# GpSimd takes the C products of steps 14 and 15 in place of step 8, y in four terms, and the first stage's softmax two row steps earlier

## The reference, cut to what matters

```python
xn = layernorm(x)
# branch 1, a selective scan (N = 16 states)
deltaBC = xn @ W_deltaBC.T                       # 64 + 16 + 16 columns
delta, B, C = split(deltaBC, [64, 80])
delta = softplus(delta @ W_dt.T + b_dt)          # [b, l, 256]
deltaA = exp(delta[..., None] * A)               # [b, l, 256, 16]
BX = delta[..., None] * B[:, :, None, :] * xn[..., None]
hs = scan over l of  h = deltaA * h + BX
y = einsum('blds,bls->bld', hs, C) + D * xn
# branch 2, 8 experts of which each picks its 128 best tokens of every batch
S = softmax(xn @ Wg.T);  G, I = top_k(S^T, 128)
out = G * (gelu(xn[I] @ W1 + b1) @ W2 + b2), added to the rows I
result = x + y + out
```

## Time and profile before

| | |
|---|---|
| median of three runs | 2423.44 us (2422.18 to 2428.61) |
| the profiled execution, device time | 2422.32 us |
| its span in the trace | 2420.4 us |
| granted TensorE clock, mean | 0.987 |
| DVE busy | 2349.7 us (97%) |
| PE busy | 2286.8 us (94%) |
| POOL busy | 2146.5 us (89%) |
| ACT busy | 2074.3 us (86%) |
| DMA, mean | 167 GB/s; near 100% of the engines in the first 120 us, 50 to 65% after |

### The profile page before, as it was taken

The page is one execution under the profiler, slowest core; times in us unless marked ns, Lnnn a source line. Parts: engine busy times, 40 slices in busy tenths (PEclk is TensorE's granted clock), DMA queues, the critical chain, the costliest instruction groups (busy, mean ns, idle before and its releaser), DMA issues. The chain is left out here.

```text
span 2420.4 us, 33772 instructions
## 1 busy us (share of the span) xinstructions
PE 2286.8 (94%) x10756; PEld 1816.4 (75%) x10756; DVE 2349.7 (97%) x1975; ACT 2074.3 (86%) x3629; POOL 2146.5 (89%) x1235
## 2 busy tenths in 40 slices
PE   7749999999999999999999999999999999999996
PEld 4437777777777777777777777777778777777775
DVE  5799999999999999999999999999999999999997
ACT  7748889898888888988888889888898989888884
POOL 5527999999999899999999999999999999999997
PEclk9969999999999999999999999999999999999998
DMA  9967575645656565555656555565646456565444
GB/s 344 338 209 266 158 221 157 177 136 148 168 147 173 145 161 141 165 154 134 184 137 173 136 166 145 141 176 143 177 127 180 127 151 163 149 173 139 128 127 79
DMA packets 151649, 403.04 MB, mean 167 GB/s; under 512 B 19536, under 2 KB 88240, under 8 KB 134832
## 3 DMA queue, kind: packets, MB, share of 16 engines
q1 hardware_dynamic: 84208, 316.72, 38.2%
q0 software_dynamic: 66048, 83.92, 20.6%
q10 hardware_dynamic: 1216, 0.23, 0.0%
HBM read 323.72 MB, written 91.75 MB: 172 GB/s over the span
## 5 line engine op out<-in xcount | busy, mean ns | idle before, releaser
L585 POOL TENSOR_TENSOR ysum<-ysum,prod 128x1024 f32<-128x1024 f32 x415 | 1121.4, 2702 | 20.3 <-DVE prod L1008 12.1
L997 DVE TENSOR_TENSOR_SCAN bank_x<-decay,bank_x 128x1024 f32<-128x1024 f32 x448 | 1024.7, 2287 | 8.9 <-DVE bank_x L936 0.5
L1163 PE MATMUL bank_l<-ext,w_sb 128*128 128x256 f32 x4096 | 968.9, 384 | 28.2 <-ACT og L757 22.6
L1229 PE MATMUL bank_l<-w_sb,hid 128*128 128x256 f32 x4096 | 939.0, 382 | 0.0
L1163 PEld LDWEIGHTS bank_l<-ext,w_sb 128*128 128x128 f32 x4096 | 760.3, 191 | 166.5 <-ACT og L757 31.0
L1229 PEld LDWEIGHTS bank_l<-w_sb,hid 128*128 128x128 f32 x4096 | 767.5, 190 | 130.0 <-issue 29.0
L717 ACT ACTIVATE decay<-delta,a_sb 128x511 f32<-128x511 f32 x1024 | 641.9, 707 | 15.8 <-POOL delta L517 14.6
L936 DVE TENSOR_TENSOR bank_x<-du,bank_b 128x1024 f32<-128x1024 f32 x512 | 617.6, 1206 | 4.7 <-ACT bank_b L748 3.2
L726 ACT ACTIVATE hid<-bank_l,b_all 128x256 f32<-128x256 f32 x1024 | 431.5, 475 | 203.8 <-PE bank_l L1163 200.7
L1008 DVE TENSOR_TENSOR prod<-bank_x,c_all 128x1024 f32<-128x1024 f32 x448 | 544.9, 1216 | 0.1
L540 POOL DMA_INDIRECT out<-og,idx_all x256 | 410.0, 1601 | 43.8 <-POOL ysum L585 42.5
(11 more groups left out here) (117 smaller groups left out, 1958.9 us busy)
## 6 DMA issues: line engine op xcount, KB each, us to landing
c_all<-bc_rows SPq DMA_DIRECT2D x128, 1024.0 KB, 5.1
b_wide<-bc_rows SPq DMA_DIRECT2D x128, 512.0 KB, 4.5
w_sb<-in_w SPq DMA_DIRECT2D x32, 1024.0 KB, 9.3
decay<-in_x SPq DMA_DIRECT2D x32, 512.0 KB, 6.8
xn_rows<-c_all SPq DMA_DIRECT2D x32, 512.0 KB, 6.5
out<-yrow POOLq DMA_DIRECT2D x32, 512.0 KB, 8.5
xr<-xn_rows SPq DMA_DIRECT2D x30, 512.0 KB, 6.0
bc_rows<-prod SPq DMA_DIRECT2D x32, 192.0 KB, 5.1
```

Of the source, the lines that this page charges most:

```text
L585: nc.gpsimd.tensor_tensor(ysum[:, m % 2], first, prod[:, i], ALU.add).then_inc(sum_done, 1)
L997: nc.vector.tensor_tensor_scan(into, decay[:, k % 2, i].rearrange("p c t -> p (c t)"), bank_x[:, s % 2], 0.0, ALU.mult, ALU.add).then_inc( ...
L1163: i = nc.tensor.matmul(bank_l[(q + v) % 2][:, (f % 2) * UT:(f % 2 + 1) * UT], w1_sb[:, e2, hc, f * P:(f + 1) * P], ext[:, v % 2, hc], star ...
L1229: i = nc.tensor.matmul(o, hid[:, w % 2, f, c * K:(c + 1) * K], w2_sb[:, w_par, f], start=False, stop=(f == FC - 1 and c == UB - 1))
```

## The change

Three things are changed.
- `GP_STEPS` is (4, 14, 15) and `KEPT` is (14, 15): POOL makes the products with C of steps 4, 14 and 15, DVE those of the 13 others (before: 14 others). Step 8 becomes an ordinary step: DVE's product, POOL's add. Steps 14 and 15 are scanned into `kept[:, 0]` and `kept[:, 1]`, multiplied there by POOL and not added by it. `kept` no longer alternates from batch to batch, so DVE waits before both scans until PE has turned all of the batch before (`y_tr`, b * 2). POOL has 13 adds and 3 products in a batch, before 14 and 2.
- y is turned in four terms instead of three: ysum, kept 0, kept 1, skip; 16 matmuls per half instead of 12. For the last batch the terms are added one at a time, each as soon as it is there, with one accumulation per half that starts with skip and ends with kept 1; the second half goes to `bank_l[0]`. Two scatters of the last unit move by a step.
- In the first stage `first` stands in the row steps 4g + 3 and takes the group that PE turned in row step 4g + 1 (before: in row step 4g + 5). `second` and the exponential come two row steps earlier too, so do `TURN0` and the start of the top-k rounds: row steps 23 to 31 hold one round each, 32 to 34 two, 35 the last.

```diff
 BODY = 4
-GP_STEPS = (4, 8)
-KEPT = 8
+GP_STEPS = (4, 14, 15)
+KEPT = (14, 15)
 BU = BODY * SLOTS
...
 WIDE = (1, 2)
-TURN0 = HALF + ROWS - 2
-EARLY = {NB - 7: (0,), NB - 6: (1,), NB - 5: (2,), NB - 4: (3,), NB - 3: (4,), NB - 2: (5,), NB - 1: (6,), NB: (7, 8),
-         NB + 1: (9, 10), NB + 2: (11, 12), NB + 3: (13, 14), NB + 4: (15,)}
+TURN0 = HALF + ROWS - 4
+EARLY = {NB - 9: (0,), NB - 8: (1,), NB - 7: (2,), NB - 6: (3,), NB - 5: (4,), NB - 4: (5,), NB - 3: (6,), NB - 2: (7,), NB - 1: (8,),
+         NB: (9, 10), NB + 1: (11, 12), NB + 2: (13, 14), NB + 3: (15,)}
 LEAD = 16
...
         def sums(s):
-            return s - (s + N - 1) // N - (s + N - 1 - KEPT) // N
+            return s - (s + N - 1) // N - sum((s + N - 1 - n) // N for n in KEPT)
         def gp_prods(s):
...
                                 pool.wait_ge(c_in[u % 2], (u // 2 + 1) * 16)
-                                from_, to = (kept[:, m % 2], kept[:, m % 2]) if n == KEPT else (state[:], prod[:, i])
+                                from_, to = (kept[:, n % 2], kept[:, n % 2]) if n in KEPT else (state[:], prod[:, i])
                                 wait(pool, sum_done, sums(s - 2))
...
                                 pool.wait_ge(gp_prod_done, gp_prods(s + 1))
-                            elif s < NB * N - 1:
+                            else:
                                 pool.wait_ge(prod_done, dve_prods(s + 1))
...
                                 first = ysum[:, m % 2]
-                            if n > 0 and n != KEPT and s < NB * N - 1:
+                            if n > 0 and n not in KEPT:
                                 nc.gpsimd.tensor_tensor(ysum[:, m % 2], first, prod[:, i], ALU.add).then_inc(sum_done, 1)
...
                             scatter(u - 1, 1)
-                        if i == 2 and u == NU - 1:
-                            scatter(u, 1)
-                            scatter(u, 0)
+                        if i in (1, 2) and u == NU - 1:
+                            scatter(u, 2 - i)
                         if i == 3 and sl == 0 and there(b - 2, NB) and u < NU:
...
                     b = q * ROWS + r
-                    g, gq = q * 2 + r // GATE, r // GATE % 2
+                    g, gp = q * 2 + r // GATE, (r // GATE + 1) % 2
                     if b == 5:
...
                         nc.scalar.copy(proj[:, (r - 3) % 4], lg_banks[(r - 3) % 2][0:PJ, :]).then_inc(proj_done, 1)
-                    if r % GATE == 1 and there(g - 2, NB // GATE):
-                        act.wait_ge(lsh_done, g - 1)
-                        nc.scalar.activation(lexp[:, gq], lsh[:, gq], ACT.Exp).then_inc(lexp_done, 1)
+                    if r % GATE == 3 and there(g - 1, NB // GATE):
+                        act.wait_ge(lsh_done, g)
+                        nc.scalar.activation(lexp[:, gp], lsh[:, gp], ACT.Exp).then_inc(lexp_done, 1)
             through(rows, NB // ROWS)
...
                 wait(act, delta_done, nb - 1)
-                wait(act, gp_prod_done, gp_prods((nb - 2) * N + KEPT) if nb > 1 else 0)
+                wait(act, gp_prod_done, gp_prods((nb - 2) * N + KEPT[0]) if nb > 1 else 0)
                 wait(act, du_done, nb - 2)
...
                     gq = 1 - gp
-                    first = r % GATE == 1 and there(g - 2, NB // GATE)
-                    second = r % GATE == 3 and there(g - 2, NB // GATE)
+                    first = r % GATE == 3 and there(g - 1, NB // GATE)
+                    second = r % GATE == 1 and there(g - 2, NB // GATE)
                     lg = bank_t[:, 0:TC * GATE * E].rearrange("p (a e) -> p a e", e=E)
                     if first:
-                        dve.wait_ge(lg_tr, g - 1)
-                        nc.vector.reduce_max(lmax[:, gq], lg, axis=AX.X).then_inc(lmax_done, 1)
+                        dve.wait_ge(lg_tr, g)
+                        nc.vector.reduce_max(lmax[:, gp], lg, axis=AX.X).then_inc(lmax_done, 1)
                     if second:
...
                     if first:
-                        dve.wait_ge(lmax_done, g - 1)
-                        nc.vector.tensor_tensor(lsh[:, gq], lg, lmax[:, gq].unsqueeze(2).broadcast_to([P, TC * GATE, E]),
+                        dve.wait_ge(lmax_done, g)
+                        nc.vector.tensor_tensor(lsh[:, gp], lg, lmax[:, gp].unsqueeze(2).broadcast_to([P, TC * GATE, E]),
                                                 ALU.subtract).then_inc(lsh_done, 1)
...
                         dve.wait_ge(bx_done, s + 1)
-                        if n == KEPT:
-                            wait(dve, y_tr, b * 2 - 2)
-                            into = kept[:, par].rearrange("p c t -> p (c t)")
+                        if n in KEPT:
+                            wait(dve, y_tr, b * 2)
+                            into = kept[:, n % 2].rearrange("p c t -> p (c t)")
                         elif n in GP_STEPS:
...
             dve.wait_ge(y_added, (NB - 2) * 16)
-            nc.vector.tensor_copy(yrow[:, (NB - 1) % 2, 2:4], bank_x[:, 0, 0:T].rearrange("p (c d) -> p c d", c=2)).then_inc(yrow_done, 1)
+            nc.vector.tensor_copy(yrow[:, (NB - 1) % 2, 2:4], bank_l[0].rearrange("p (c d) -> p c d", c=2)).then_inc(yrow_done, 1)
         @block.tensor
...
                 pe.wait_ge(skip_done, y + 1)
-            def y_rows(par, half, last=False):
-
-                into = bank_x[:, 0, 0:T] if last and half else bank_t[:]
+            def y_rows(par, half):
+
                 for c in (2 * half, 2 * half + 1):
                     for dt in range(HC):
-                        part = into[:, (c % 2) * D + dt * P:(c % 2) * D + (dt + 1) * P]
+                        part = bank_t[:, (c % 2) * D + dt * P:(c % 2) * D + (dt + 1) * P]
                         rows = slice(c * P, (c + 1) * P)
-                        terms = [ysum[:, par, dt, rows], kept[:, par, dt, rows], skip[:, par, dt, rows]]
-                        if last:
-                            terms.append(prod[:, STEPS - 1, dt, rows])
+                        terms = (ysum[:, par], kept[:, 0], kept[:, 1], skip[:, par])
                         for t, term in enumerate(terms):
-                            o = nc.tensor.matmul(part, term, ident[:], start=(t == 0), stop=(t == len(terms) - 1), is_transpose=True)
+                            o = nc.tensor.matmul(part, term[:, dt, rows], ident[:],
+                                                 start=(t == 0), stop=(t == len(terms) - 1), is_transpose=True)
                 o.then_inc(y_tr, 1)
+
+            def last_term(term, half, first=False, last=False):
+
+                into = bank_l[0] if half else bank_t[:]
+                for c in (2 * half, 2 * half + 1):
+                    for dt in range(HC):
+                        o = nc.tensor.matmul(into[:, (c % 2) * D + dt * P:(c % 2) * D + (dt + 1) * P],
+                                             term[:, dt, c * P:(c + 1) * P], ident[:],
+                                             start=(first and c % 2 == 0 and dt == 0), stop=(last and c % 2 == 1 and dt == HC - 1), is_transpose=True)
+                return o
             def spread_b(s, n, par):
...
                                 y_rows((m - 1) % 2, 0)
-                        if q in (5, 6) and u == NU:
+                        if q == 5 and u == NU:
+                            par = (NB - 1) % 2
                             pe.wait_ge(yrow_done, NB * 2 - 2)
-                            pe.wait_ge(sum_done, sums(NB * N) - 1)
+                            pe.wait_ge(og_done, NU * UB)
+                            pe.wait_ge(skip_done, NB)
+                            for half in range(2):
+                                last_term(skip[:, par], half, first=True)
+                            pe.wait_ge(sum_done, sums(NB * N))
+                            for half in range(2):
+                                last_term(ysum[:, par], half)
+                            pe.wait_ge(gp_prod_done, gp_prods(NB * N) - 1)
+                            for half in range(2):
+                                last_term(kept[:, 0], half)
                             pe.wait_ge(gp_prod_done, gp_prods(NB * N))
-                            pe.wait_ge(prod_done, dve_prods(NB * N))
-                            pe.wait_ge(skip_done, NB)
-                            y_rows((NB - 1) % 2, q - 5, True)
+                            for half in range(2):
+                                last_term(kept[:, 1], half, last=True).then_inc(y_tr, 1)
             through(main, NJ)
```

## The result

| | before | after |
|---|---|---|
| median of 4 runs | 2423.74 us (2422.18 to 2428.61) | 2440.56 us (2439.20 to 2441.17) |
| profiled execution's span | 2420.4 us | 2438.5 us |

After stands to before as 1.0065, 95% interval 1.0048 to 1.0083: the change made the kernel slower, by some 16 us, and the time lies above the predicted range (2409 to 2438).

The account below looks back on a forecast made before the run. DVE and POOL were both taken as full, with the ring within 1 us. Terms -7.8 - 1.0 + 6 + 0.9 + 0.4 = -1.5 us gave 2420.8; with the median 1.1 above, 2422 us, no change, range 2409 to 2438.

Parts of the forecast that it names:

- DVE's part: Main stage: one more short step per batch saves 0.90 us; DVE alone would take 68.5 us per batch.
- POOL's part: Main stage: a shorter gap ahead of the gather and small extra costs sum to -0.35 us, 69.05 us per batch.
- the ring: Main stage: chain of waits from DVE over PE's matmuls and ACT's work back to DVE; 69.05 to 69.15 us after the change.
- PE's part: Main stage: sixteen turning matmuls instead of twelve take 0.44 us more per half; the second half costs 0 to 0.1 us.
- DVE's new wait: Main stage: DVE's wait for the turned y before scans 14 and 15 costs nothing, with 6 us of cover.
- SP's list: Main stage: C and B loads go out at about 10 us of the batch; cost nothing, 1 us of cover for B.
- rival 3: Main stage: B for slot 1 lands late and ACT waits, half a microsecond per batch, +15 us, 2437 us; chance 0.18.
- First stage: Before the first scan: DVE stalls for PE's turned logits every four row steps; +6 us, bounds -4.5 and +10.
- Last batch and end: Batch 31 and after: 32 matmuls in place of 24 cost +0.9 us, POOL's last products and scatters +0.4.
- Rival 2: First stage: DVE finds the turned logits in time and two rounds go into idle time, -4.5 us; 2411 us; chance 0.16.
- Rival 4: POOL's gap ahead of the gather stays 0.80 us and first-stage stalls cost 10 us; 2434 us; chance 0.08.
- rival 1: Main stage: DVE is the bound and its 0.90 us per batch are paid in full; 2402 us; chance 0.10.

Follow-up runs that it names:

- x3_both_less: e1_main_only with both POOL's add of step 9 cut to 8 of 512 columns and PE's turned term of step 15 left out; 2399.29 us, ratio 0.9892.
- x2_one_term_less: e1_main_only with PE leaving the kept product of step 15 out of the turned y of batches 0 to 30; 2418.30 us, ratio 0.9973.
- x1_pool_less: e1_main_only with POOL's add of step 9 cut to 8 of 512 columns in every batch; 2414.69 us, ratio 0.9957.
- e1_main_only: The changed kernel with the first stage of the kernel before; 2414.24 us, ratio 0.9964.
- e9_both_short: Changed kernel; from row step 10 PE's logits use half the channels and ACT normalises 8 of 256 columns in two of three chunks; 2426.05 us, ratio 1.0011.
- e4_one_up: The changed kernel with softmax, rounds and their transpose one row step up instead of two; 2415.37 us, ratio 0.9967.
- e5_copies_later: The changed kernel with four copies of x issued in slots 1 and 2 of batch 0, behind those slots' loads; 2433.52 us, ratio 1.0040.
- e7_max_behind: The changed kernel with the softmax's maximum and shift behind that row step's bn_stats, shift and bn_aggr on DVE; 2418.18 us, ratio 0.9977.
- e6_short_xn: The changed kernel with ACT normalising only 8 of 256 columns in one of a row's three chunks from row step 9; 2437.70 us, ratio 1.0054.

## Why the prediction was wrong

**DVE's part: right.** It put DVE alone at 68.5 us per batch from the earlier trace rows; x3_both_less shows 68.4.

**POOL's part: right.** The 0.52 us of the gap went as said, and the extra 0.10 came (0.28 against 0.17 us). With the ring relieved x2_one_term_less shows 69.03 where 69.05 was reckoned. That POOL was full could not be read from its busy share (89% before, 88% after), only from the lag.

**PE's part and the ring: right in mechanism, 0.1 us too dear.** The ring alone gives 69.03 (x1_pool_less), just under the low end of 69.05 to 69.15. I took the high end because two nested loops "cost a little"; they cost nothing that shows. Over batches 1 to 30 the whole step was forecast at -8.5 and came to -9.2 (-11.3 in e1_main_only). That these agree so well is partly luck. Steady batches gained 0.31 us by their median, not 0.25, and the -1.0 us for DVE's lead over POOL did not come in these batches: from batch 1 to batch 31 the lag of POOL's first add grew from 10.2 to 12.2 us before, and from 11.7 to 13.4 after.

**DVE's new wait, SP's list: right.** No wait of DVE behind the turned y stands in its rows. ACT waited for B 1.5 us over 16 batches, so rival 3's half microsecond per batch is 0.1. Only in batch 0 does its sign show, ACT waiting for `b_wide` in slot 1, and there the copies cause it, not POOL's product.

**First stage: here the prediction failed.** The stall, its place and its loop of 5.6 us were as said (7.5 us across the stall on ACT, where 5.75 + 2.0 was reckoned). Wrong was the term "3 x 2.15 us" for the row steps between two stalls. 2.15 us is DVE's own work per row step, but DVE does not pace these steps: it ends them early and then waits 7.5 us. ACT's own list does, at 2.9 to 3.6 us, with PE's logits in one of the three (e9_both_short and the table of row steps above). With 3.3 in that place the same sum gives 5.75 + 2.0 + 3 x 3.3 = 17.7 us, where 17.4 was measured. So row step 23 began at 100.9 us, not at 88.0. From there on the forecast holds again: 60.2 us to the end of the last softmax were forecast (88.0 to 148.2), and it ends at 160.6, 59.7 us after row step 23. The price was in the trace of before, where ACT's rows never start less than 2.84 us apart once the first two are done:

```profile
32.29 1.58 ACT L654 ACTIVATE c_all<-decay,hid 128x256 f32<-128x256 f32 x3
...
35.14 1.59 ACT L654 ACTIVATE c_all<-decay,hid 128x256 f32<-128x256 f32 x3
```

I had read only the 15 us per four row steps at which the DMAs hold them there. Whether that is a floor for a kernel that runs late is not shown: e9_both_short ran at 14.3 to 14.8 and e4_one_up at 14.0 in the same stretch, but both were behind the kernel before, whose fifth turn starts first of the three (85.4, 86.0 and 90.4 us).

**Batch 0: not in the sum.** The prediction followed the first stage up to the first scan and passed the delay on "in full". But SP's list hangs on the last rows, not on DVE's rounds. Before, its first copies went out 144.16 - 140.92 = 3.2 us ahead of DVE's first work behind the rounds; after, 2.0 us behind it (164.45 against 162.45), and the second four copies moved from 1.4 us ahead of the batch's first scan to 4.1 us behind it, ahead of the loads of slot 1. e5_copies_later took 6.7 us off this batch.

**Last batch and end: mis-sized, +2.9 for +1.3.** From the start of the add of step 12 to DVE's copy the forecast was 19.0 us and 2429.66 - 2410.89 = 18.8 came. But that add itself stands 2.5 us later in the batch: 0.95 for the 32 matmuls, as forecast; 0.7 for DVE's wait ahead of step 1, which I counted in the 69.05 of the other batches and forgot in this one; and 0.9 because the short step now is 14, behind step 12, and no longer 8, ahead of it.

**The rivals.** None of them happened as priced. Rival 2 was right that moving softmax costs nothing by itself (e7_max_behind, e4_one_up), but its gain isn't there either: the first scan stays at 181. Rival 4 priced the stalls highest, at 10 us, still 8 short. In the first stage the mechanism was in the prediction and only its price was wrong; the 6 us of batch 0 were in no rival.

The rule quoted for rival 1 from the Trainium skill ("Perfetto Trace Analysis", Optimizing Scalar/DVE Operations), that with DVE saturated work may go to GpSimd, holds here in sign: e1_main_only is 0.36% faster. By x1_pool_less to x3_both_less it is GpSimd's own full list and the ring together that keep the gain at some 0.35 of the 0.90 us.

## What to carry to other kernels

When an edit makes an engine wait sooner, list what stands behind the wait in that engine's order, and ask whether the thing waited for needs any of it: e7_max_behind has the same early softmax as the kernel after and 18 us less, by the place of one wait. Price the steps between such stalls by the engine with the longest list in them, here ScalarE, not by the work of the one that stalls. When a stage's end moves, check what hangs on its other outputs, here the bulk copies that fell in front of the first urgent loads; and when two limits stand at the same number, taking away either shows nothing, so test them together before calling one harmless.

## What the runs showed of the hardware

- A DMA issued right behind others pays for them: B issued at 207.3 us let ACT start only 18 us later, behind 4 MB of copies and 1 MB of C, while the page's median to landing was 4.5 us before. Issued at 207.4 us with those copies behind it, ACT did not wait for it, 12 us later.
- TensorE's granted clock fell over the idle time of a stall and stayed low at its next work: 0.50 between 69 and 74 us in e6_short_xn, where four matmuls of logits took 3.33 us against 1.88 us in the next row; in the kernel after, eight turning matmuls took 1.91 us at 69.59 and 1.04 us at 73.92. The kernel before has 1.00 from 20 to 90 us.
- GpSimd's gap ahead of an indirect DMA is 0.27 to 0.28 us when the DMA itself carries the wait for GpSimd's last product, and 0.80 us where a wait for its last result came first (before).
- Relieving VectorE of a product of 1.22 us frees 0.90 us of its time (69.3 without its waits before, 68.4 in x3_both_less), as the step lengths of the earlier trace rows say.
- ScalarE's normalisation of a chunk of 256 columns and one of 8 differ by only 0.2 us, of some 0.55: most of such a small instruction does not depend on its columns.
